# Second attention of a two-layer transformer kernel: row sums by the exponentials' accumulator, later projections, masked queries on GpSimd

## The chip, the cores and the metric

The kernel runs on one core of a Trainium2 chip. The metric is the device time of one execution in microseconds (us). The kernel before takes 2906.33 us (median of three, 2905.99 to 2908.69).

## What is computed

Two layers on x of 32 x 256 tokens x 128. Each layer adds attention and a feed-forward part (mixture of experts) of the normalised input to the residual. The change touches only the second layer's attention: 16 heads of 8 channels, causal, with a bias that falls with distance.

```python
q, k, v = (proj(q_w), proj(k_w), proj(v_w))
scores = jnp.einsum('bhid,bhjd->bhij', q, k) / scale
scores = scores - distance[None] * _slopes(N_HEADS)[:, None, None]
scores = jnp.where(causal[None, None], scores, -jnp.inf)
attn = jax.nn.softmax(scores, axis=-1)
out = jnp.einsum('bhij,bhjd->bhid', attn, v)
out = out.transpose(0, 2, 1, 3).reshape(b, l, D_MODEL)
return out @ o_w
```

## The kernel before

The program has four stages, one after the other: the first feed-forward part, the first attention, the second layer's experts, and the second attention, in which the experts' rows are also gathered and added. Everything is 32-bit floating point.

The second attention goes over 32 batches (sequences). A batch is eight units: two halves of 128 queries times four sets of four heads. Units 0 to 3 are narrow (the first 128 queries see 128 keys), units 4 to 7 wide (256 keys). Four units of one half make a group, whose context is gathered in one bank, O_ps. Five queues run beside one another, and each walks the same hand-written list of steps s (STEPS); in a step each does its part for a different unit, and semaphores hold them together:

- TensorE in step s: turn(s-1) transposes the exponentials (L1478, four transposes narrow, eight wide), value(s-2) multiplies them with v into columns 0 to 127 of O_ps (L1496) and with a table of ones into columns 128 to 255, which gives the row sums, turned and repeated over each head's channels (L1500), score(s+1) makes the scores (L1466), then comes a projection if the list has one.
- VectorE in step s: at s % 4 == 2 it divides a finished group: reciprocal of the sums (L1405), product (L1409). Then four minimum passes over the scores of unit s, which add the bias and give the negated scores and their minimum (L1419, each followed by a read of the accumulator), then the copy of the first half of the transposed unit s-1 (L1427). After an output projection it adds the total (L1434).
- ScalarE in step s: four exponentials of unit s (L1388), for wide units the copy of the second transposed half of s-1 (L1395), then it empties the projection bank: four masked copies of the queries, one per head position (L1367), kT (L1368), or v (L1377).
- GpSimd: indirect gathers of the experts' rows (L1335), the weighting and two sums (L1348, L1352, L1357). The last of them waits until the output projection two batches back was added.
- SyncE: loads of the transposed input (behind the v projection two batches back), stores of the output.

All projections share one bank, M_ps, in the order of job_list: q and k of the next batch at step 8b+1, v at 8b+2, the output projection of the batch before at 8b+3. Each waits until the bank was emptied of the one before (spare_free).

The lines of the list and of the division:

```python
job_list += [(UB * b + 1, "qk", b + 1), (UB * b + 2, "v", b + 1)]
job_list += [(UB * b + 3, "out", b - 1)]
dve.reciprocal(rinv[g % 2][:, :], O_ps[:, P:2 * P]).then_inc(inverted, 1)
```

Of the kernel before, what the change touches and what calls it, by code (L numbers as in the profile page):

```python
# [31 lines left out]
P = 128  # L32
S = 256
D = 128
H = 16
C = 8
# [25 lines left out]
def program(nc, io, nb, cap):  # L62
# [5 lines left out]
    with ctx:  # L68
# [434 lines left out]
        with ExitStack() as pm:  # L503
# [10 lines left out]
            UB = 8  # L514
# [575 lines left out]
        v_of = [sb(f"v1_heads{i}", [P, KT, 4, D]) for i in range(2)]  # L1090
        one_of = sb("ones_heads", [P, 4, 32])
        zeros_set = sem("zeros_set")
        ones_set = sem("ones_set")
        alibi_built = sem("alibi_built")

        with ExitStack() as pc:
# [27 lines left out]
            with nc.Block() as block:  # L1124
# [93 lines left out]
                def _(pool):  # L1218
# [3 lines left out]
                    for i in range(2):  # L1222
                        pool.memset(v_of[i][:, :, :, :], 0.0).then_inc(zeros_set, 1)
                    pool.memset(one_of[:, :, :], 0.0).then_inc(zeros_set, 1)
                    pool.wait_ge(zeros_set, 3)
                    for i in range(4):
                        pool.memset(one_of[:, i, C * i:C * i + C], 1.0).then_inc(ones_set, 1)
                    for h in range(H):
# [9 lines left out]
        with ExitStack() as pb:  # L1238
# [14 lines left out]
            xt = [sbb(f"xt1_{i}", [P, S]) for i in range(2)]  # L1253
            q_of = [sbb(f"q1_heads{i}", [P, 4, S]) for i in range(2)]
            kT = [sbb(f"kT1_{i}", [P, S]) for i in range(2)]
# [4 lines left out]
            rinv = [sbb(f"rinv1_{i}", [P, P]) for i in range(2)]  # L1260
            ctxT = [sbb(f"ctxT1_{i}", [P, S]) for i in range(2)]
# [14 lines left out]
            moved1 = semb("probsT_second_half_moved")  # L1276
            valued = semb("values_ready")
            inverted = semb("inverse_sums_ready")
            normed = semb("context_ready")
            spare_full = semb("spare_full")  # L1280
            spare_free = semb("spare_free")
            rows_weighted = semb("expert_rows_weighted")
            one_added = semb("first_expert_added")
# [15 lines left out]
            for b in range(nb + 1):  # L1299
                if b + 1 < nb:  # L1300
                    job_list += [(UB * b + 1, "qk", b + 1), (UB * b + 2, "v", b + 1)]
                if b >= 1:
                    job_list += [(UB * b + 3, "out", b - 1)]
            job_no = {(name, b): n + 1 for n, (_, name, b) in enumerate(job_list)}
            jobs_at = {}
            for s, name, b in job_list:
                jobs_at.setdefault(s, []).append((name, b))
            STEPS = range(-2, UB * nb + 7)

# [21 lines left out]
            def _(pool):  # L1331
                def gather(b):
                    for i in range(2):
                        for k in range(2):
                            pool.indirect_dma_start(out=expert_rows[b % 2][:, i, k, :], out_offset=None, in_=expert_out,  # L1335
                                                    in_offset=bass.IndirectOffsetOnAxis(ap=slot_ids[:, 2 * b + i, k:k + 1], axis=0)
                                                    ).then_inc(gathered[b % 2], 16)

                gather(0)
                for b in range(nb):  # L1340
# [5 lines left out]
                    if b >= 1:  # L1346
# [5 lines left out]
                    pool.tensor_tensor(with_one[:, :, :], weighted[:, :, 0, :], residual[:, 2 * b:2 * b + 2, :],  # L1352
                                       ALU.add).then_inc(one_added, 1)
                    pool.wait_ge(one_added, b + 1)
                    if b >= 2:
# [5 lines left out]
            def _(act):  # L1361
                def move(name, b):
                    n = job_no[name, b]
                    if name == "qk":
                        act.wait_ge(spare_full, n)
                        for i in range(4):
                            act.mul(q_of[b % 2][:, i, :], M_ps[:, 0:S], cview["head_scale"][:, i:i + 1])  # L1367
                        act.copy(kT[b % 2][:, :], M_ps[:, S:2 * S]).then_inc(spare_free, 1)  # L1368
                    elif name == "v":
                        act.wait_ge(spare_full, n)  # L1370
                        if b < 2:
                            act.wait_ge(zeros_set, 3)
                        else:
                            act.wait_ge(valued, UB * (b - 1))
# [25 lines left out]
            def _(dve):  # L1400
                for s in STEPS:
                    if s >= 6 and s % 4 == 2 and s // 4 - 1 < 2 * nb:
                        g = s // 4 - 1
                        dve.wait_ge(valued, 4 * (g + 1))
                        dve.reciprocal(rinv[g % 2][:, :], O_ps[:, P:2 * P]).then_inc(inverted, 1)  # L1405
                        dve.wait_ge(inverted, g + 1)
                        if g >= 4:
                            dve.wait_ge(spare_full, job_no["out", g // 2 - 2])
                        dve.tensor_tensor(ctxT[g // 2 % 2][:, g % 2 * P:(g % 2 + 1) * P], O_ps[:, 0:P], rinv[g % 2][:, :],  # L1409
                                          ALU.mult).then_inc(normed, 1)  # L1410
# [27 lines left out]
            def _(pe):  # L1438
# [42 lines left out]
                def value(u):  # L1481
# [4 lines left out]
                    if i == 0 and g >= 1:  # L1486
                        pe.wait_ge(normed, g)
                    if u == 0:
                        pe.wait_ge(ones_set, 4)
                    if u % UB == 0:  # L1490
                        pe.wait_ge(spare_free, job_no["v", b])
                    n = half_of(u) + 1
                    for kt in range(n):
                        for j in range(4):
                            rows = slice(32 * j, 32 * j + 32)
                            pe.matmul(O_ps[rows, 0:P], v_of[b % 2][:, kt, i, rows], probsT[u % 3][:, kt, j, :],  # L1496
                                      start=(i == 0 and kt == 0), stop=(i == 3 and kt == n - 1), skip_group_check=True)
# [89 lines left out]
```

## Time and profile before

| | |
|---|---|
| median of three | 2906.33 us |
| profiled execution by itself | 2909.2 us |
| its span | 2907.5 us |
| mean granted clock of TensorE | 0.969 |
| busy: TensorE, VectorE, ScalarE, GpSimd | 90%, 66%, 55%, 21% |
| second attention | 2180 us to the end |

The page gives busy time and instructions by engine, the span in 40 slices with the granted clock of TensorE in tenths of full speed, and the chain of work that ended last. The chain can be read in order of time: each piece is what the end waited for at that time. The timeline shows every engine, with the idle time before an instruction and what ended it in brackets. A matmul in 32-bit is recorded as two instructions, a transpose as one.

### The profile page before, as it was taken

The numbers are of one execution on the slowest core, as the hardware profiler recorded it, in microseconds if no ns is written. First come the engines' busy times: TensorE is split into PE (matmuls) and PEld (weight loads), VectorE is DVE, ScalarE is ACT, GpSimd is POOL, SyncE is SP. The second block draws the span as 40 slices with busy tenths as digits, with TensorE's granted clock in tenths as the row PEclk, the third lists the DMA queues.
The fourth block names the chain that finished last, engine by engine and source line by source line (L and its number), as shares of the span: only waits on it lengthen the run. The fifth ranks groups of instructions, "written<-read, shape, count | busy, mean of one in ns | idle before, by whom it ended". The sixth has DMA issues, their size and how long they took to land. (4 is left out here: it accounts for less than half of the span.)

```text
span 2907.5 us, 102728 instructions
## 1 busy us (share of the span) xinstructions
PE 2604.1 (90%) x42000; PEld 1971.0 (68%) x42000; DVE 1924.4 (66%) x7310; ACT 1611.4 (55%) x3731; POOL 613.6 (21%) x632
## 2 busy tenths in 40 slices
PE   4999999799988999999999999499989999998998
PEld 3777777567767777777777777377766666666666
DVE  4887788467777777777777777211117777777777
ACT  1444444366666666666666665133327666767776
POOL 2445444300110000001111111400004223322230
PEclk9999999899999999999999999699999999999999
DMA  3212100166666666666666665222321001111110
GB/s 131 103 51 73 37 15 12 36 152 148 154 151 149 152 153 148 152 155 149 152 150 153 150 149 123 86 84 98 101 72 35 24 24 29 26 24 24 28 27 9
DMA packets 341502, 268.43 MB, mean 92 GB/s; under 512 B 24602, under 2 KB 328090, under 8 KB 339516
## 3 DMA queue, kind: packets, MB, share of 16 engines
q1 hardware_dynamic: 330556, 234.82, 31.4%
q0 software_dynamic: 10496, 27.28, 3.2%
q8 instruction: 323, 5.29, 0.8%
q14 instruction: 127, 1.04, 0.1%
HBM read 129.88 MB, written 132.14 MB: 90 GB/s over the span
## 5 line engine op out<-in xcount | busy, mean ns | idle before, releaser
L869 DVE CUSTOM_DVE_ANT_0 neg_scores<-scores,rel_bias 128x256 f32<-128x256 f32 x1024 | 373.4, 421 | 271.7 <-PE scores L1013 226.4
L1388 ACT ACTIVATE probs<-neg_scores,low 128x256 f32<-128x256 f32 (+1 forms) x1024 | 382.5, 446 | 211.6 <-DVE low L1419 187.4
L757 ACT ACTIVATE probs<-neg_scores,low 128x256 f32<-128x256 f32 x1024 | 436.8, 500 | 42.9 <-DVE low L869 41.8
L751 ACT COPY probsT_s<-probsT 128x512 f32<-128x512 f32 x256 | 150.3, 587 | 427.6 <-PE probsT L1025 427.6
L1419 DVE CUSTOM_DVE_ANT_0 neg_scores<-scores,alibi 128x256 f32<-128x256 f32 (+1 forms) x1024 | 304.8, 354 | 109.5 <-PE scores L1466 109.2
L1025 PE MATMUL probsT<-consts,probs 128*128 128x128 f32 x2048 | 332.7, 286 | 1.3 <-ACT probsT_s L751 0.7
L1025 PEld LDWEIGHTS probsT<-consts,probs 128*128 128x128 f32 x2048 | 229.1, 143 | 72.9 <-issue 59.4
L252 POOL TENSOR_TENSOR hid<-hid,gate_bc 128x512 f32<-128x512 f32 x160 | 205.4, 1284 | 275.8 <-DVE hid L407 257.3
L876 DVE COPY rel_s<-scores 128x768 f32<-128x768 f32 x256 | 244.0, 953 | 3.0 <-PE scores L1013 1.6
L1003 PE MATMUL scores<-k_sides,q_heads 32*128 32x256 f32 x2048 | 184.3, 429 | 55.6 <-DVE rel_s L876 54.1
L1478 PE MATMUL probsT<-consts,probs 128*128 128x128 f32 x1536 | 226.8, 285 | 3.7 <-ACT probs L1388 0.4
L1427 DVE COPY probsT_s<-probsT 128x512 f32<-128x512 f32 x256 | 175.9, 687 | 68.6 <-PE probsT L1478 68.4
L1041 PE MATMUL values<-probsT_s,v_heads 128*32 128x128 f32 x4096 | 216.1, 283 | 0.8 <-issue 0.8
L1188 ACT ACTIVATE he<-up,b1e 128x512 f32<-128x512 f32 (+1 forms) x192 | 112.0, 616 | 183.4 <-PE up L1166 183.2
L1478 PEld LDWEIGHTS probsT<-consts,probs 128*128 128x128 f32 x1536 | 172.7, 144 | 56.3 <-ACT probs L1388 39.0
L1045 PE MATMUL values<-probsT_s,ones_heads 128*32 128x128 f32 x4096 | 209.6, 276 | 0.0
L1213 DVE TENSOR_TENSOR ye<-down,b 128x512 f32<-128x512 f32 (+1 forms) x48 | 28.9, 603 | 253.0 <-PE down L1174 253.0
L712 POOL TENSOR_TENSOR scat_f<-dumpk,sk 128x8 f32<-128x8 f32 x16 | 3.1, 195 | 888.4 <-DVE dump_at L849 888.4
L275 ACT ACTIVATE th<-gate_up 128x512 f32<-128x512 f32 x160 | 95.8, 599 | 168.5 <-PE gate_up L464 166.7
L484 PE MATMUL ffn_down<-weights,hid 128*128 128x128 f32 x1280 | 184.0, 287 | 0.1
L484 PEld LDWEIGHTS ffn_down<-weights,hid 128*128 128x128 f32 x1280 | 156.8, 192 | 36.3 <-issue 27.7
L719 POOL DMA_INDIRECT packed<-xn,scat x128 | 124.2, 970 | 268.1 <-DVE low L869 243.8
(187 smaller groups left out, 5158.9 us busy)
## 6 DMA issues: line engine op xcount, KB each, us to landing
rel_rows<-rel_s SPq DMA_DIRECT2D x256, 192.0 KB
rel_bias<-rel_rows SPq DMA_DIRECT2D x256, 192.0 KB, 4.0
rel_rows<-rel_s SPq DMA_DIRECT2D x256, 128.0 KB
rel_bias<-rel_rows SPq DMA_DIRECT2D x256, 128.0 KB, 3.4
packed<-ffn_in SPq DMA_DIRECT2D x8, 1280.0 KB, 5.5
xe<-packed SPq DMA_DIRECT2D x16, 640.0 KB, 4.3
expert_out<-ye POOLq DMA_DIRECT2D x16, 640.0 KB, 6.9
xt<-xnT SPq DMA_DIRECT2D x64, 128.0 KB, 3.1
```

Of the source, the lines that this page charges most:

```text
L252: pool.tensor_tensor(hid[p % 2][:, k, :], hid[p % 2][:, k, :], gate_bc[m % 3][:, :], ALU.mult).then_inc(hid_done, 1)
L484: ins = pe.matmul(D_ps[p % 2][:, i * D:(i + 1) * D], hid[p % 2][:, k, i * P:(i + 1) * P], wview["wdown"][:, k * D:(k + 1) * D], start=(k = ...
L757: act.activation(probs[s % 2][:, j, :], neg[s % 2][:, j, :], ACT.Exp, bias=low[s % 3][:, j:j + 1], scale=-1.0).then_inc(exped, 1)
L869: dve.tensor_tensor_reduce(neg[s % 2][:, j, :], S_ps[:, 512 * j:512 * j + S], bias_of(s)[:, j, :], 1.0, 3e38, ALU.add, ALU.min, low[s % 3] ...
L876: dve.tensor_copy(rel_s[u % 2][:, :, :], S_ps[:, :].rearrange("p (j w) -> p j w", j=4)[:, :, S:S + 3 * R]).then_inc(rel_moved, 1)
L1003: ins = pe.matmul(S_ps[:, 512 * j:512 * j + S], q_of[b % 2][rows, i, qt * P:(qt + 1) * P], k_of[b % 2][rows, qt, :], start=True, stop=True)
L1025: ins = pe.transpose(PT_ps[:, j * P:(j + 1) * P], probs[u % 2][:, j, kt * P:(kt + 1) * P], ident)
L1041: pe.matmul(O_ps[rows, qt * P:(qt + 1) * P], v_of[b % 2][:, kt, i, rows], pt[:, j, :], start=(u % UB == 0 and kt == 0), stop=(i == 3 and k ...
L1045: ins = pe.matmul(O_ps[rows, S + qt * P:S + (qt + 1) * P], one_of[:, i, :], pt[:, j, :], start=False, stop=(i == 3 and kt == KT - 1), skip ...
L1388: act.activation(probs[s % 3][:, j, 0:w], neg[s % 3][:, j, 0:w], ACT.Exp, bias=low[s % 3][:, j:j + 1], scale=-1.0).then_inc(exped, 1)
L1419: dve.tensor_tensor_reduce(neg[s % 3][:, j, 0:w], S_ps[j][:, 0:w], alibi[:, 4 * j + i, S - w:S], 1.0, 3e38, ALU.add, ALU.min, low[s % 3][: ...
L1478: ins = pe.transpose(PT_ps[kt][:, j * P:(j + 1) * P], probs[u % 3][:, j, kt * P:(kt + 1) * P], ident)
```

## The change

1. The ones table, its memsets and the ones matmuls go. Each exponential gets accum_out, which leaves its row sum in a 128 x 4 x 4 tile of the group. Behind the copy of a group's last unit VectorE takes the reciprocal of 128x16 sums and widens them to 128x128 (each head's value repeated over its eight channels). TensorE turns this with one matmul against the identity into columns 128 to 255 of O_ps, behind the last values of the group. At the old place of the reciprocal stands a copy of these columns to SBUF; the product follows as before.
2. The v projection moves from step 8b+2 to 8b+3, the output projection from 8b+3 to 8b+5.
3. ScalarE copies the queries once (q_raw); GpSimd makes the four masked copies (query_heads), for batch 0 ahead of its first gather, for later ones behind with_one. The scores of a batch's first unit wait for q_ready.

```diff
-                job_list += [(UB * b + 1, "qk", b + 1), (UB * b + 2, "v", b + 1)]
+                job_list += [(UB * b + 1, "qk", b + 1), (UB * b + 3, "v", b + 1)]
-                job_list += [(UB * b + 3, "out", b - 1)]
+                job_list += [(UB * b + 5, "out", b - 1)]
...
+                def query_heads(b):
+                    pool.wait_ge(spare_free, job_no["qk", b])
+                    for i in range(4):
+                        ins = pool.tensor_scalar(q_of[b % 2][:, i, :], q_raw[:, :], cview["head_scale"][:, i:i + 1], None, ALU.mult)
+                    ins.then_inc(q_ready, 1)
+
+                query_heads(0)
                 gather(0)
...
+                    if b >= 1:
+                        query_heads(b)
                     pool.wait_ge(one_added, b + 1)
...
-                        for i in range(4):
-                            act.mul(q_of[b % 2][:, i, :], M_ps[:, 0:S], cview["head_scale"][:, i:i + 1])
+                        if b >= 1:
+                            act.wait_ge(q_ready, b)
+                        act.copy(q_raw[:, :], M_ps[:, 0:S])
...
+                        g, i = s // 4, s % 4
+                        if i == 0 and g >= 2:
+                            act.wait_ge(inverted, g - 1)
...
                             act.activation(probs[s % 3][:, j, 0:w], neg[s % 3][:, j, 0:w], ACT.Exp,
-                                           bias=low[s % 3][:, j:j + 1], scale=-1.0).then_inc(exped, 1)
+                                           bias=low[s % 3][:, j:j + 1], scale=-1.0,
+                                           accum_out=sums[g % 2][:, j, i:i + 1]).then_inc(exped, 1)
...
-                        dve.reciprocal(rinv[g % 2][:, :], O_ps[:, P:2 * P]).then_inc(inverted, 1)
-                        dve.wait_ge(inverted, g + 1)
+                        dve.tensor_copy(rinvT[:, :], O_ps[:, P:2 * P]).then_inc(inverse_moved, 1)
+                        dve.wait_ge(inverse_moved, g + 1)
...
+                        if u % 4 == 3:
+                            g = u // 4
+                            dve.wait_ge(exped, 16 * (g + 1))
+                            dve.reciprocal(rinv[:, :], sums[g % 2][:, :, :].rearrange("p j i -> p (j i)")).then_inc(one_inverse, 1)
+                            dve.wait_ge(one_inverse, g + 1)
+                            if g >= 1:
+                                dve.wait_ge(valued, 4 * g)
+                            dve.tensor_copy(rinv_c[:, :, :], rinv[:, :].unsqueeze(2).to_broadcast((P, H, C))).then_inc(inverted, 1)
...
                     if u % UB == 0:
                         pe.wait_ge(spare_free, job_no["qk", b])
+                        pe.wait_ge(q_ready, b + 1)
...
-                        for j in range(4):
-                            rows = slice(32 * j, 32 * j + 32)
-                            ins = pe.matmul(O_ps[rows, P:2 * P], one_of[:, i, :], probsT[u % 3][:, kt, j, :],
-                                            start=False, stop=(i == 3 and kt == n - 1), skip_group_check=True)
+                    if i == 3:
+                        pe.wait_ge(inverted, g + 1)
+                        ins = pe.matmul(O_ps[:, P:2 * P], rinv_c[:, :, :].rearrange("p h c -> p (h c)"), ident, start=True, stop=True)
                     ins.then_inc(valued, 1)
```

## Rows read from the trace of the kernel before

**Rows 1.** The page, part 2: TensorE's granted clock in 40 slices.
```profile
PEclk9999999899999999999999999699999999999999
```
**Rows 2.** Chain in order of time, longest pieces: start us, us, what.
```profile
2285.22 1.15 PE projected L1454 x4
...
2868.85 1.15 PE projected L1454 x4
```
**Rows 3.** The same chain from 2485 to 2545 us, all pieces.
```profile
2495.75 1.13 PE probsT L1478 x8
2496.88 0.36 PE values L1496 x8
2497.24 0.22 PE values L1500 x8
...
2497.89 0.43 PE scores L1466 x8
2498.32 1.02 PE probsT L1478 x8
...
2500.79 0.59 PE probsT L1478 x4
...
2502.82 0.63 PE projected L1445 x2
...
2507.79 0.44 PE probsT L1478 x4
...
2508.80 0.69 PE scores L1466 x8
...
2517.27 1.13 PE probsT L1478 x8
...
2530.93 1.17 PE scores L1466 x8
...
2540.30 1.13 PE probsT L1478 x8
```
**Rows 4.** Timeline, one batch: start us, us, engine, line, out<-in, [idle before <-releaser].
```profile
2504.04 1.28 ACT L1388 ACTIVATE probs<-neg_scores,low 128x128 f32<-128x128 f32 x4 [1.50 <-DVE low L1419]
...
2505.23 1.54 ACT L1367 ACTIVATE q_heads<-projected,consts 128x256 f32<-128x256 f32 x4
...
2507.08 0.71 PE L1449 MATMUL projected<-weights,xt 128*128 128x128 f32 x4 [1.75 <-ACT kT L1368]
...
2513.81 0.95 DVE L1405 RECIPROCAL rinv<-values 128x128 f32<-128x128 f32 x1
...
2514.11 1.12 PE L1478 MATMUL probsT<-consts,probs 128*128 128x128 f32 x8
...
2514.79 0.29 DVE L1409 TENSOR_TENSOR ctxT<-values,rinv 128x128 f32<-128x128 f32 x1
...
2515.00 0.41 DVE L1419 CUSTOM_DVE_ANT_0 neg_scores<-scores,alibi 128x256 f32<-128x256 f32 x1
...
2515.34 0.08 DVE L1419 DVE_READ_ACCUMULATOR2_ANT low<- 128x1 f32 x1
2515.34 0.42 DVE L1419 CUSTOM_DVE_ANT_0 neg_scores<-scores,alibi 128x256 f32<-128x256 f32 x1
...
2515.52 1.71 ACT L1388 ACTIVATE probs<-neg_scores,low 128x256 f32<-128x256 f32 x4 [0.99 <-DVE low L1419]
```
**Rows 5.** Groups by line and shape: count, busy us, mean ns, idle before.
```profile
L1395 ACT COPY probsT_s<-probsT 128x512 f32<-128x512 f32 x128 | 72.1, 563 | 0.7 <-PE probsT L1478 0.7
...
L829 DVE RECIPROCAL gk<-den 128x4 f32<-128x4 f32 x16 | 2.9, 179 | 0.5
```
**Rows 6.** Timeline of ScalarE in the first stage, two small instructions.
```profile
328.32 0.21 ACT L297 ACTIVATE ex<-gap 128x4 f32<-128x4 f32 x1
328.42 0.20 ACT L298 ACTIVATE sg<-logit 128x4 f32<-128x4 f32 x1
```
**Rows 7.** Timeline of GpSimd in the experts' stage, sixteen tensor_scalar.
```profile
1856.09 14.65 POOL L1229 TENSOR_SCALAR alibi<-consts 128x256 f32<-128x256 f32 x16
```

More of the change, by code:

```diff
@@ L1090, in program @@
         v_of = [sb(f"v1_heads{i}", [P, KT, 4, D]) for i in range(2)]
-        one_of = sb("ones_heads", [P, 4, 32])
         zeros_set = sem("zeros_set")
-        ones_set = sem("ones_set")
         alibi_built = sem("alibi_built")
@@ L1223, in _ @@
                         pool.memset(v_of[i][:, :, :, :], 0.0).then_inc(zeros_set, 1)
-                    pool.memset(one_of[:, :, :], 0.0).then_inc(zeros_set, 1)
-                    pool.wait_ge(zeros_set, 3)
-                    for i in range(4):
-                        pool.memset(one_of[:, i, C * i:C * i + C], 1.0).then_inc(ones_set, 1)
                     for h in range(H):
@@ L1254, in program @@
             q_of = [sbb(f"q1_heads{i}", [P, 4, S]) for i in range(2)]
+            q_raw = sbb("q1_raw", [P, S])
             kT = [sbb(f"kT1_{i}", [P, S]) for i in range(2)]
@@ L1259, in program @@
             probsT = [sbb(f"probsT1_s{i}", [P, KT, 4, P]) for i in range(3)]
-            rinv = [sbb(f"rinv1_{i}", [P, P]) for i in range(2)]
+            sums = [sbb(f"sums1_{i}", [P, 4, 4]) for i in range(2)]
+            rinv = sbb("rinv1", [P, H])
+            rinv_c = sbb("rinv1_c", [P, H, C])
+            rinvT = sbb("rinv1_T", [P, P])
             ctxT = [sbb(f"ctxT1_{i}", [P, S]) for i in range(2)]
@@ L1277, in program @@
             valued = semb("values_ready")
+            one_inverse = semb("inverse_sums_of_heads")
             inverted = semb("inverse_sums_ready")
+            inverse_moved = semb("turned_inverse_moved")
             normed = semb("context_ready")
@@ L1281, in program @@
             spare_free = semb("spare_free")
+            q_ready = semb("query_heads_ready")
             rows_weighted = semb("expert_rows_weighted")
@@ L1307, in program @@
                 jobs_at.setdefault(s, []).append((name, b))
-            STEPS = range(-2, UB * nb + 7)
+            STEPS = range(-2, UB * nb + 8)
             block = pb.enter_context(nc.Block())
@@ L1365, in move @@
                         act.wait_ge(spare_full, n)
-                        for i in range(4):
-                            act.mul(q_of[b % 2][:, i, :], M_ps[:, 0:S], cview["head_scale"][:, i:i + 1])
+                        if b >= 1:
+                            act.wait_ge(q_ready, b)
+                        act.copy(q_raw[:, :], M_ps[:, 0:S])
                         act.copy(kT[b % 2][:, :], M_ps[:, S:2 * S]).then_inc(spare_free, 1)
@@ L1371, in move @@
                         if b < 2:
-                            act.wait_ge(zeros_set, 3)
+                            act.wait_ge(zeros_set, 2)
                         else:
@@ L1404, in _ @@
                         dve.wait_ge(valued, 4 * (g + 1))
-                        dve.reciprocal(rinv[g % 2][:, :], O_ps[:, P:2 * P]).then_inc(inverted, 1)
-                        dve.wait_ge(inverted, g + 1)
+                        dve.tensor_copy(rinvT[:, :], O_ps[:, P:2 * P]).then_inc(inverse_moved, 1)
+                        dve.wait_ge(inverse_moved, g + 1)
                         if g >= 4:
                             dve.wait_ge(spare_full, job_no["out", g // 2 - 2])
-                        dve.tensor_tensor(ctxT[g // 2 % 2][:, g % 2 * P:(g % 2 + 1) * P], O_ps[:, 0:P], rinv[g % 2][:, :],
+                        dve.tensor_tensor(ctxT[g // 2 % 2][:, g % 2 * P:(g % 2 + 1) * P], O_ps[:, 0:P], rinvT[:, :],
                                           ALU.mult).then_inc(normed, 1)
@@ L1487, in value @@
                         pe.wait_ge(normed, g)
-                    if u == 0:
-                        pe.wait_ge(ones_set, 4)
                     if u % UB == 0:
@@ L1495, in value @@
                             rows = slice(32 * j, 32 * j + 32)
-                            pe.matmul(O_ps[rows, 0:P], v_of[b % 2][:, kt, i, rows], probsT[u % 3][:, kt, j, :],
-                                      start=(i == 0 and kt == 0), stop=(i == 3 and kt == n - 1), skip_group_check=True)
-                        for j in range(4):
-                            rows = slice(32 * j, 32 * j + 32)
-                            ins = pe.matmul(O_ps[rows, P:2 * P], one_of[:, i, :], probsT[u % 3][:, kt, j, :],
-                                            start=False, stop=(i == 3 and kt == n - 1), skip_group_check=True)
+                            ins = pe.matmul(O_ps[rows, 0:P], v_of[b % 2][:, kt, i, rows], probsT[u % 3][:, kt, j, :],
+                                            start=(i == 0 and kt == 0), stop=(i == 3 and kt == n - 1), skip_group_check=True)
+                    if i == 3:
+                        pe.wait_ge(inverted, g + 1)
+                        ins = pe.matmul(O_ps[:, P:2 * P], rinv_c[:, :, :].rearrange("p h c -> p (h c)"), ident, start=True, stop=True)
                     ins.then_inc(valued, 1)
```

## The prediction

> **What bounds the kernel now.** I read the page first: the clock line, which stays at nine tenths and over in the last quarter [rows 1]. The second attention, which alone is changed, fills the last quarter: from the first projection at 2180 us to the end. Then the chain of the whole span: the same output projection stands in it at 2285.22 and, 26 batches later, at 2868.85 [rows 2], so a batch of eight units takes (2868.85 - 2285.22) / 26 = 22.45 us. Then one batch of the chain in order of time [rows 3]; the time from the start of one transposition of a unit to the next is a step. From unit 6 of a batch at 2495.75 to unit 6 of the next at 2517.27 it is 21.52 us. With units counted 0 to 7 and steps named by the unit that is transposed, step 6 takes 2.57 (to 2498.32), step 7 2.47 (to 2500.79), steps 0 and 1 7.0 (to 2507.79), steps 2 to 4 6.3 (to 2514.11) and step 5 3.2 [rows 3, 4].
>
> TensorE sets steps 6, 7, 0 and 2 to 4 nearly alone: its pieces follow one another in the chain. Step 7, for instance, is 1.02 (eight transposes) + 0.36 + 0.22 + 0.22 + 0.22 (values and ones, two key halves) + 0.43 (scores) = 2.47 [rows 3]. Step 1 is long because the v projection waits 1.75 us for the copies of ScalarE (four masked queries, 1.54 us, then kT) [rows 4]. Step 5 is set by VectorE: the reciprocal starts at 2513.81 and the next unit's minimum pass only at 2515.00, 1.19 us later [rows 4]. After each such row I ask what would be late next, for the gain ends there.
>
> The difference between 21.52 and 22.45 is the clock: in every second batch TensorE shows a stretch at its lower level (1.2 GHz), right behind the idle 1.75 us before the v projection. The scores of one unit then take 1.17 instead of 0.69 [rows 3]. The batch after the one above takes 23.03 (2517.27 to 2540.30), so some 1.5 us per pair, 0.75 per batch.
>
> **Part 1, the ones matmuls.** They go, 0.22 us of TensorE for each key half in the chain [rows 3]. Four narrow units have one half, four wide ones two: 12 x 0.22 = 2.6 us per batch. In their place comes one full matmul per group of four units; the two of the v projection with their issue take 0.71 [rows 4], so about 0.3 each, 0.6 per batch. Net -2.0 us of TensorE.
>
> **Part 2, the row sums.** Each of the 32 exponentials of a batch gets an accumulator read on ScalarE. The trace has none there, and this is the price on which everything hangs. Call it a, per exponential, on ScalarE's throughput. Bounds: on VectorE each minimum pass is followed by such a read of 0.08, and the next pass starts at the same instant, 2515.34 [rows 4]: a = 0 from below. From above, the dearest small ScalarE instruction (128x4) takes 0.21 by itself: a = 0.21 [rows 6]. In between, two such small instructions back to back start 0.10 apart [rows 6]. I take 0.10, since the read is to be expected as an instruction of its own of that size in the same queue. A gain below nothing is excluded: no work of ScalarE's exponential goes away.
>
> **Part 3, the division.** VectorE loses two reciprocals of 128x128 per batch (0.95 each) and gets, per group, a reciprocal of 128x16 (128x4 takes 0.18, 128x128 takes 0.95 [rows 4, 5]; with some 6.2 ns per element 0.25), a widening copy and a copy of the turned sums, each 128x128; their bounds are 0.18, the tiny instruction, and 0.95, the reciprocal, and I take the 0.29 of the product, which is nearest in shape and work [rows 4]. At the critical place, ahead of unit 6's and unit 2's minimum pass, 1.19 becomes 0.5 (a copy, and a product whose end overlaps the next pass). The other 0.5 stands behind the copy of unit 3's and 7's transpositions. The added matmul waits for it. Behind that wait on TensorE stand the scores of the unit two steps later and, through them, VectorE and ScalarE; but the sums are ready 1.2 us after the last minimum pass of that step, while the transposes (0.5 to 1.1, begun 0.6 behind that pass) and the values end later, so the wait costs nothing. If that cover were gone it would cost up to 0.5 twice a batch, 32 us in all.
>
> **Part 4, the queries.** ScalarE's four products (1.54 [rows 4]) become one copy, a quarter of that (0.38): -1.15 us per batch. GpSimd gets four tensor_scalar of 128x256. Sixteen of them took 14.65 us [rows 7], so 3.7 us per batch. They stand in its queue behind the gathers and the first two sums (some 7 us), so they are done about four steps after the queries' copy; scores need them six steps after, with some 5 us left over. What queues behind them (the second sum of the experts' rows) is needed 13 steps later. If the cover were gone, each us of lateness costs one per batch. Only at the start is it bare: the first scores wait for 0.38 + 3.7 instead of 1.54, so +2.3 us once; the first gathers move behind it and have time.
>
> **Part 5, the projections' places.** With v at step 3 of a batch, its wait for ScalarE (copy and kT, two copies of that size, 0.75 behind the exponentials of unit 2) lies beside transposes, values and scores (1.55). The 1.75 us go. The output projection moves with it and stands in step 4; the loads on SyncE's queue wait for v and out and are issued ten units ahead, two more matter not.
>
> **The sum.** For each step I take the largest of what TensorE, ScalarE and VectorE have to do and of the latency from scores to the transposition. That latency is, wide: 0.05 + 0.52 (first minimum to first exponential) + 1.71 + 0.05 = 2.33 and four reads; narrow 1.76 and four reads [rows 4]. The same method on the kernel before gives back the steps above within 0.1. After:
> - step 6: TensorE 1.13 + 0.58 (values of two key halves, 0.36 + 0.22) + 0.43 = 2.1, latency 2.4 + 4a: **2.8**
> - step 7: TensorE 2.0, ScalarE (copy 0.56 [rows 5], four narrow exponentials) 1.95 + 4a: **2.35**
> - steps 0 and 1: TensorE 2.85 (with the q and k projection) + 1.3: **4.2**; ScalarE 3.75 + 8a hides
> - step 2: TensorE 2.1, ScalarE (0.75 + 1.28 + gaps) + 4a: **2.5**
> - step 3: TensorE 1.55, ScalarE and latency 1.8 + 4a: **2.2**
> - steps 4 and 5: TensorE 3.1 (with the added matmul and the output projection) + 2.4: **5.5**; VectorE 2.0 + 2.9 and ScalarE 5.0 + 4a hide
>
> Together 19.55 us per batch against 22.45, and the clock's 0.75 is in this difference: I count it as gained, because the idle piece ahead of the lower clock goes and no idle piece in my table is over 0.7. So 2.9 x 31.5 batches = -91, +2.3 at the start, -1 at the end (shorter division), -89.5. The profiled execution took 2909.2 by itself (its span 2907.5), 2.9 more than the median of 2906.33; 2909.2 - 89.5 - 2.9 gives **2817**. By the ends of a: at 0 the steps are 2.4, 2.05, 4.15, 2.2, 1.7, 5.5 = 18.0, so 2768; at 0.21 ScalarE has 15.4 us of its own work and 32 x 0.21 = 6.7, 22.1, so 2897.
>
> **A rule that speaks against it.** The widening copy on VectorE goes from SBUF to SBUF while GpSimd makes queries; the trace of before has no such pair in this stage, VectorE's copies here come from PSUM. Were the copy held for a whole GpSimd instruction (0.85 to 0.92 [rows 7]) once a batch, it would fall in step 3, where 0.5 of it is hidden: up to 0.4 x 32 = 13 us. The Trainium skill (SBUF — State Buffer, "Who interferes with whom") says that a VectorE copy in a two-port mode and GpSimd lock each other out of a shared port pair for a whole instruction. No row here shows it; by it the sum would be at most 2830, inside the range.
>
> **The rivals.**
> - *The read is hidden* (a under 0.05), as on VectorE: 2768 to 2792. For it the row of VectorE's reads; against it that small ScalarE instructions do take their 0.10.
> - *ScalarE becomes the bound* (a from 0.14 to 0.21): 2845 to 2897. TensorE then waits for exponentials in nearly every step. For it: ScalarE's own work is 15.4 us per batch already (four wide exponentials at 1.71, four narrow at 1.28 less the overlaps, four copies at 0.6, queries, kT and v 1.2).
> - *Slower than before*: the read overlaps neither the exponential before it (0.10 lost) nor the one behind (0.21 [rows 6]): a = 0.31, 15.4 + 9.9 = 25.3 us per batch, 2.9 x 31.5 = +91, 2997. It decides from a = 0.22 on, where ScalarE's 15.4 + 32a passes 22.45. Against it: neighbouring instructions on ScalarE overlap [rows 6].
> - *It doesn't do what it says*: the queries come late, or the lower clock stays. TensorE has 17.4 us of work in 19.6, 89%, where it has 19.4 in 22.45 now, 86%; so I doubt it, but falls of the clock may go on at 0.75 per batch: +24, 2841. Late queries by over 5 us would give back 1 us of each batch per us.
>
> **How the numbers follow.** Chances: my case (a from 0.05 to 0.14, 2792 to 2845) 0.45; hidden read 0.24; ScalarE bound 0.17; slower 0.07; queries late or clock low for long stretches, 2870 to 2910, 0.07. The range runs from 2768 to 2880: it leaves out the slower case, half of the last one and the dear end of ScalarE's. A measurement of this kernel tells 0.2%, 6 us, from no change. Faster: 0.45 + 0.24 + 0.17 + 0.04 = 0.90, same 0.03, slower 0.07.
>
> **What would show it.** Right: reads on ScalarE, with exponentials of a wide unit standing 0.50 apart instead of 0.40; no idle time of TensorE before the v projection; 1.2 us less between VectorE's copies around unit 6, no reciprocal of 0.95; a batch of 19 to 20 us; the wait for the turned sums absent from the list of waits. Wrong: exponentials 0.6 apart; TensorE waiting for GpSimd's queries; VectorE's small copy far over 0.3; a clock line in the last quarter lower than before.

## The result

The changed kernel takes 2797.7 us (median of four, 2797.55 to 2800.91) against 2906.16 (four, 2905.67 to 2908.69): a ratio of 0.9628, 95% interval 0.9611 to 0.9644, 108 us or 3.7% faster. The prediction was 2817 us with a range from 2768 to 2880. The profiled execution has a span of 2799.2.

The page of the changed kernel: span, busy times, TensorE's clock in 40 slices.

```profile
span 2799.2 us, 98114 instructions
...
PE 2515.8 (90%) x39056; PEld 1887.1 (67%) x39056; DVE 1912.2 (68%) x7438; ACT 1668.0 (60%) x4659; POOL 730.2 (26%) x755
...
PEclk9999999989999999999999999979999899999999
```

Against [rows 1] the clock line looks alike, since a slice of it rounds. The table by stretches of the second attention shows the difference (us from the start, length, busy times of TensorE, weight loads, VectorE, ScalarE and GpSimd, granted clock, DMA share, GB/s), first the kernel before, then the changed one:

```profile
2400.00:2500.00 100.00, 91.14 (x1424) 65.50 (x1425) 76.34 (x344) 70.60 (x192) 31.20 (x35) 0.95 0.11 29
```

```profile
2400.00:2500.00 100.00, 93.18 (x1179) 63.33 (x1177) 88.54 (x431) 92.61 (x383) 53.62 (x59) 1.00 0.11 28
```

The clock is 1.00 where the kernel before has 0.95 in the same stretch, and three engines are now about equally busy. One batch of the chain in order of time answers to [rows 3]:

```profile
2488.59 1.13 PE probsT L1502 x8
2489.72 0.57 PE values L1518 x16
2490.30 0.43 PE scores L1490 x8
2490.73 0.59 PE probsT L1502 x4
2491.32 0.57 PE values L1518 x16
2491.89 0.42 PE values L1522 x2
...
2493.80 0.44 PE probsT L1502 x4
...
2495.11 0.63 PE probsT L1502 x4
...
2498.41 1.08 ACT probs L1402 x4
2499.50 0.04 issue
2499.54 1.10 PE probsT L1502 x8
...
2502.70 0.87 PE probsT L1502 x8
...
2506.38 1.09 ACT probs L1402 x4
2507.47 0.04 issue
2507.51 1.13 PE probsT L1502 x8
```

From the transposition of unit 7 at 2488.59 to the next at 2507.51 it is 18.92 us. The values of unit 7 take 0.57 without ones (L1518), then stands the one added matmul (L1522, 0.42). No piece of VectorE's division is left in the chain; before, the reciprocal stood in it ahead of unit 6. The chain now leaves TensorE ahead of the transpositions of units 4 and 7 (2499.54 and 2507.51), where it goes through ScalarE's exponentials. 22.45 - 18.92 = 3.53 us per batch, by 31.5 batches 111, less 2.6 lost at the start: that is the 108.

How the comparisons below are made. The experiments were measured in four series, each beside the kernel before: e1 to e4; e5, e6, e7 and e9; e10, e11 and e8; e12. In three of these, with nine of the twelve runs, some steps of each batch are longer for every kernel whose trace was kept, and the kernel before takes 2992 to 2999 us instead of 2902 to 2906. I call this the long step. It lies where GpSimd issues its four gathers or just behind: steps 5 and 6 with the projections at their old places, steps 7 and 0 at the new ones (in e7 nearly all of it in step 7). With the lower clock around it a batch is 2 to 5 us longer in the mean. So the totals of these runs can't be set against the 2797.7. The last batch that is followed by another (from the transposition of unit 0 to the next unit 0) has no gathers in it and no long step, and in the series without long steps it is as long as the others (18.92 in the changed kernel, in e10 and in e11). Its length, read from TensorE's timeline, is what I compare. It is one batch of one execution per kernel; where the same kernel was profiled again it came out the same within 0.01 us (18.92 three times, 18.17 in e4 and e12). The columns are the units' steps, from the start of one transposition to the next, and the batch, in us; the last column is TensorE's granted clock in that batch:

| kernel | 0 | 1 | 2 | 3 | 4 | 5 | 6 | 7 | batch | clock |
|---|---|---|---|---|---|---|---|---|---|---|
| before | 3.00 | 3.91 | 3.38 | 2.21 | 2.43 | 3.16 | 2.50 | 2.47 | 23.06 | 0.93 |
| before, batch at full clock | 3.00 | 3.91 | 2.30 | 1.88 | 2.31 | 3.16 | 2.50 | 2.47 | 21.52 | 1.00 |
| changed | 2.98 | 1.48 | 2.16 | 2.27 | 2.99 | 2.24 | 2.74 | 2.06 | 18.92 | 1.00 |
| e1, before with reads | 3.00 | 4.74 | 3.38 | 2.25 | 2.31 | 3.27 | 2.51 | 2.47 | 23.93 | 0.93 |
| e2, before, positions | 3.00 | 1.66 | 2.88 | 1.80 | 2.85 | 2.74 | 2.50 | 2.46 | 19.89 | 1.00 |
| e3, before, queries | 3.00 | 2.72 | 2.29 | 1.88 | 2.31 | 3.16 | 2.50 | 2.47 | 20.33 | 1.00 |
| e12, changed without reads | 2.98 | 1.47 | 2.16 | 1.90 | 2.99 | 2.18 | 2.43 | 2.06 | 18.17 | 1.00 |
| e5, changed, old positions | 2.98 | 2.40 | 2.08 | 2.26 | 2.71 | 2.53 | 2.55 | 2.05 | 19.56 | 1.00 |
| e6, changed, ScalarE's queries | 2.98 | 1.47 | 3.10 | 1.97 | 2.99 | 2.25 | 2.73 | 2.06 | 19.55 | 1.00 |
| e7, changed with ones too | 3.42 | 1.53 | 2.36 | 2.26 | 3.21 | 2.62 | 2.79 | 2.50 | 20.69 | 1.00 |
| e9, changed, more ScalarE | 3.05 | 1.61 | 2.46 | 2.35 | 2.99 | 2.54 | 2.82 | 2.41 | 20.22 | 1.00 |
| e8, output at step 7 | 2.98 | 1.48 | 2.16 | 2.27 | 2.44 | 2.79 | 2.61 | 1.98 | 18.71 | 1.00 |

### The profile page after: what moved, and what is told of

Read it like the earlier page. It is cut to its first block and busy times, and to the rows that moved or that the text cites. A ratio compares the mean times of both kernels' runs of the same rounds, so it can differ in the third digit from the quotient of the medians.

```text
span 2799.2 us, 98114 instructions
## 1 busy us (share of the span) xinstructions
PE 2515.8 (90%) x39056; PEld 1887.1 (67%) x39056; DVE 1912.2 (68%) x7438; ACT 1668.0 (60%) x4659; POOL 730.2 (26%) x755
## 3 DMA queue, kind: packets, MB, share of 16 engines
q14 instruction: 138, 1.13, 0.1%
## 5 line engine op out<-in xcount | busy, mean ns | idle before, releaser
L1402 ACT ACTIVATE probs<-neg_scores,low 128x256 f32<-128x256 f32 (+1 forms) x1024 | 453.1, 443 | 54.6 <-DVE low L1434 52.0
L1402 ACT ACTIVATION_READ_ACCUMULATOR probs<-neg_scores,low 128x1 f32 x1024 | 191.2, 187 | 0.0
```

## The experiments

In the cuts of the edits below, allocations and the length of the list of steps are left out. Theory: the gain is the wait before the v projection with the lower clock behind it, the ones matmuls, and the reciprocal ahead of units 2 and 6, less a small price of the accumulator reads, which counts only where ScalarE ends the chain. Rivals: the reads are free or dear; the ones matmuls were hidden; the clock does not hang on the wait.

### e1: the reads alone

```diff
-  bias=low[s % 3][:, j:j + 1], scale=-1.0).then_inc(exped, 1)
+  bias=low[s % 3][:, j:j + 1], scale=-1.0,
+  accum_out=sums[s // 4 % 2][:, j, s % 4:s % 4 + 1]).then_inc(exped, 1)
```

> The kernel before, with the row sums also written by the exponentials' accumulator, and not used. Theory: a read adds 0.09 us to each exponential and TensorE's chain already ends on exponentials in the steps of units 6, 4, 5 and 1, so some 4 x 0.37 us per batch come on top: 2906 + 45, 2935 to 2965. Rival: ScalarE is busy only 70% of this stage, so 32 x 0.09 = 3 us per batch disappear in its idle time: under 2916.

Measured: 3016.47 us against 2998.8 beside it, ratio 1.006 (1.0031 to 1.009), and 23.93 - 23.06 = +0.87 per batch. Both batches hold a stretch at the lower clock. Neither expectation is met: the price is there, at somewhat over half the 1.5 per batch of the theory. Nearly all of it (0.83) is in step 1, behind which ScalarE still has the four query products; in the steps of units 4 and 6, where I had put a third of it each, TensorE and VectorE hide it.

### e2: the positions alone

```diff
-  job_list += [(UB * b + 1, "qk", b + 1), (UB * b + 2, "v", b + 1)]
+  job_list += [(UB * b + 1, "qk", b + 1), (UB * b + 3, "v", b + 1)]
-  job_list += [(UB * b + 3, "out", b - 1)]
+  job_list += [(UB * b + 5, "out", b - 1)]
```

> The kernel before with only the projections moved (v three units and the output five units into a batch). Theory: TensorE's wait of 1.75 us before the v projection goes, but the four products of ScalarE (1.54 us) then delay the next exponentials, which gives some of it back; with the idle piece the stretch at the lower clock goes too (0.75 per batch): -1.9 us per batch, 2845 (2830 to 2865), the granted clock of the stage 1.00. Rival, the clock does not depend on that wait: clock as before at 0.95 to 0.97 and 2870 or more. Rival, the products bound the step as much as the wait did: 2890 or more.

Measured: 2961.55 us, ratio 0.9877 (0.9825 to 0.9929), a batch of 19.89 at a clock of 1.00: -1.63 against a batch at full clock, -2.56 against the mean of 22.45. The theory had -1.9 with the clock's part, so by this one batch it holds and is too small. Step 1 falls from 3.91 to 1.66, step 2 grows by 0.58 (the query products now delay unit 3's exponentials), and step 5 falls too, from 3.16 to 2.74, which I had not foreseen; that more of VectorE's division then lies beside TensorE's work is likely, but not shown. The total does not confirm it: ratio and clock are those of the rival (0.9877 of 2906 is 2870, and its 30 batches have 18 falls of the clock). TensorE's granted clock, read batch by batch, tells more than the mean: in the kernel before all 18 falls of the clock in its batches 1 to 30 (counted from 0) come in steps 1 and 2, right behind the wait before the v projection; in e2 all 18 come in steps 7 and 0, at the long step, and none behind the v projection. So moving the projections took the falls away from that place, and the long step, which the kernel of the result did not have, made others.

### e3: the queries alone

```diff
-  for i in range(4):
-      act.mul(q_of[b % 2][:, i, :], M_ps[:, 0:S], cview["head_scale"][:, i:i + 1])
+  if b >= 1:
+      act.wait_ge(q_ready, b)
+  act.copy(q_raw[:, :], M_ps[:, 0:S])
```

with query_heads on GpSimd as in the change.

> The kernel before with only the masked queries moved to GpSimd. Theory: the wait before the v projection becomes 1.15 us shorter, 0.6 instead of 1.75, and the lower clock goes with it; +2.3 us at the start: 2906 - 37 - 24 + 2 = 2847. Without the clock's part 2871. Rival: GpSimd is late, or its work slows VectorE: 2895 or more, with TensorE or VectorE idle until GpSimd.

Measured: 2951.29 us, ratio 0.9842 (0.9791 to 0.9893), a batch of 20.33 at a clock of 1.00: -1.19, all in step 1 (3.91 to 2.72), and -2.12 with the clock. Without the clock the theory holds to 0.04 in this batch. The total is 47.5 us shorter, not the 59 expected: here too the 30 batches have 18 falls of the clock, all of them in steps 5 to 7, at the long step, and none behind the wait of 0.6 us that is left before the v projection. In this stage no engine waits for GpSimd's queries but once, at the start.

### e4 and e12: the changed kernel without the reads

```diff
-  bias=low[s % 3][:, j:j + 1], scale=-1.0,
-  accum_out=sums[g % 2][:, j, i:i + 1]).then_inc(exped, 1)
+  bias=low[s % 3][:, j:j + 1], scale=-1.0).then_inc(exped, 1)
```

The sums are set to one on GpSimd once, so the division does nothing and the output is not the reference's.

> The changed kernel without the accumulator reads: the sums are constants set once, so the division is by ones and the output is not the reference's; all else stays. Theory: the read costs only where the latency from scores to transposes or ScalarE's queue ends last (the steps of units 6, 7, 2 and 3), about 1.0 us of 18.9 per batch: 2766 (2755 to 2775). Rival: TensorE bounds it all the same, over 2790. Rival: ScalarE bounds every step, then all 32 x 0.09 = 3.0 us per batch come back: 2702.

> The changed kernel without the accumulator reads once more (the sums are constants, the output is not the reference's), for a chip without the long step. Theory, by the undisturbed steps of the run e4_after_no_reads: 2.98 + 1.47 + 2.16 + 1.90 + 2.99 + 2.18 + 2.42 + 2.06 = 18.16 us per batch against 18.92, so 2797.7 - 0.76 x 31.5 = 2774. Rival: the disturbed steps hid a gain of ScalarE's, then all 3.0 us per batch come back, 2703.

Both series had the long step: 2926.27 us (ratio 0.9756, 0.9676 to 0.9837) and 2927.92 (0.9775, 0.9745 to 0.9804), so the totals decide nothing, and 2774 was not seen. The undisturbed batch is 18.17 in both: the reads cost 0.75 us of 18.92. TensorE's timeline of e12, its steps of units 5, 6 and 7:

```profile
2892.30 1.09 PE L1506 MATMUL probsT<-consts,probs 128*128 128x128 f32 x8
2894.73 1.12 PE L1506 MATMUL probsT<-consts,probs 128*128 128x128 f32 x8 [0.17 <-ACT probs L1405]
2896.79 0.65 PE L1506 MATMUL probsT<-consts,probs 128*128 128x128 f32 x4
```

Unit 6's step is 2.43 instead of 2.74, and TensorE's wait in it is 0.17 instead of 0.54; unit 3's is 1.90 instead of 2.27. Step 7, where I had put 0.3, does not move. By 31.5 batches that is 24 us. The rival with all 3 us is out, and so is the one of over 2790: 2797.7 less 24 is 2774, by this estimate.

### e5, e6, e7: one part taken back from the changed kernel

e5 is the diff of e2 the other way round, e6 that of e3. e7 puts the ones matmuls back ahead of the added one (with their table, not shown):

```diff
+  for j in range(4):
+      rows = slice(32 * j, 32 * j + 32)
+      ins = pe.matmul(O_ps[rows, P:2 * P], one_of[:, i, :], probsT[u % 3][:, kt, j, :],
+                      start=False, stop=(i == 3 and kt == n - 1), skip_group_check=True)
```

> The changed kernel with the projections back at their old places (v two units into a batch, the output three). Theory: TensorE waits for the copies of queries and kT again, 0.7 us instead of 1.9 since the masked queries are gone, some 0.5 us per batch: 2815 (2805 to 2825), the clock still 1.00 as the idle piece is short. Rival: the lower clock comes back with the wait and it costs 0.5 + 0.75 per batch, 2838 or more. Rival: the places are worth nothing once the queries are on GpSimd, under 2802.

> The changed kernel with the four masked query products back on ScalarE. Theory: ScalarE gets 1.15 us per batch behind the exponentials of unit 2, and unit 3's exponentials end last there: +1.0 to 1.15 per batch, -2.3 at the start: 2829 (2820 to 2835). Rival: with the v projection a unit later there is room, under 2810.

> The changed kernel with the ones matmuls put back beside the new sums (their result is overwritten). Theory: 2.6 us more of TensorE per batch, of which the waits for exponentials in the steps of units 6 and 3 hide some 0.6: +2.0 per batch, 2861 (2850 to 2872). Rival: ScalarE bounds the stage now and TensorE's work is hidden: under 2820.

Measured: e5 2904.36 (ratio 0.972, 0.9658 to 0.9782), e6 2963.62 (0.9907, 0.9878 to 0.9935), e7 2963.79 (0.9899, 0.9855 to 0.9943). By the batch: old positions +0.64, with the clock still at 1.00, as expected (0.5); ScalarE's queries +0.63, between the 1.0 of the theory and the rival's 0.4, since 0.94 more in step 2 comes back as 0.30 less in step 3; ones matmuls +1.77 against 2.0. In e7 the chain shows them at their full price beside the values (L1527, 0.22 for each key half):

```profile
2940.24 0.36 PE values L1523 x8
2940.59 0.22 PE values L1527 x8
2940.81 0.22 PE values L1523 x8
2941.03 0.22 PE values L1527 x8
2941.25 0.43 PE scores L1493 x8
```

So of the 2.6 us of these matmuls 0.8 are hidden now, most of it in steps 3 and 6, where TensorE waits for exponentials.

Two of these totals say more than their batches. e5 and e6 were measured side by side and have the same undisturbed batch (19.56 and 19.55), but e5 takes 2904 us and e6 2964. They differ in the projections' places and in which engine masks the queries. e2 and e3, measured side by side, show the same: e2 has the shorter undisturbed batch (19.89 against 20.33) and takes 10 us more. Where the long step occurs, kernels with the new places lost more to it (3.2 to 5.2 us per batch in the mean) than those with the old ones (1.9 to 3.6). So the gain of 3.7% is one for executions without the long step; with it the changed kernel's gain is probably smaller, since e4 and e12 had only 2.4 and 2.2% even without the reads.

Taken back one by one the parts are worth 0.64 (places), 0.63 (queries) and 1.77 (ones) less 0.75 for the reads, 2.29 us per batch, and the clock's part is some 0.9. Of the 3.53 this leaves some 0.3 for the new division and for what the parts give only together. No run takes the division back alone, so its own share is not shown.

### e9: more of ScalarE's time

```diff
   accum_out=sums[g % 2][:, j, i:i + 1]).then_inc(exped, 1)
+  act.copy(small[:, s, j, :], cview["head_scale"][:, :])
```

> The changed kernel with one more small ScalarE instruction (a copy of 128x4) behind each exponential, 0.10 us each, as if the read cost 0.19. Theory: ScalarE's queue becomes the bound in nearly every step, 15.4 + 32 x 0.19 = 21.5 plus some waits, 22.0 us per batch against 18.9: 2896 (2880 to 2906). Rival: the slope stays that of the other direction, about 1 us per batch per 0.09: 2835.

Measured: 3012.32 us, ratio 1.0054 (1.0024 to 1.0084), with the long step; a batch of 20.22, +1.30. The theory's 22.0 is refuted. ScalarE's timeline of e9 (start us, length):

```profile
2980.03 0.51 ACT L1403 ACTIVATE probs<-neg_scores,low 128x256 f32<-128x256 f32 x1
2980.44 0.19 ACT L1403 ACTIVATION_READ_ACCUMULATOR probs<-neg_scores,low 128x1 f32 x1
2980.53 0.18 ACT L1406 COPY small<-consts 128x4 f32<-128x4 f32 x1
2980.61 0.51 ACT L1403 ACTIVATE probs<-neg_scores,low 128x256 f32<-128x256 f32 x1
```

The added copy moves the next exponential by 0.09 (0.58 apart, and 0.49 in the changed kernel below), 2.9 us per batch, of which 1.3 arrive. The rival is met: it had 1.2 per batch. The reason is the term for ScalarE's own work, next section.

### e10, e11, e8: the changed kernel again, without gathers, and with a later output projection

e11 leaves the gathers out from the third batch on. e8:

```diff
-  job_list += [(UB * b + 5, "out", b - 1)]
+  job_list += [(UB * b + 7, "out", b - 1)]
```

> The changed kernel once more, on the chip of the next two. In the runs so far one step of each batch, the one in which GpSimd issues its four gathers, is 2 to 4 us longer than on the first chip, whatever the kernel. Theory, that this belongs to the chip: on such a chip the step of unit 7 takes 4 to 5 us instead of 2.06, the other steps are as on the first chip, 2797.7 + 32 x 2.7 = 2884 (2870 to 2900); on a chip like the first 2798. Rival, that the edited kernels made it: 2798 on any chip.

> The changed kernel without the gathers of experts' rows from the third batch on (the rows of the first two are used again, so the output is not the reference's). Theory, that the gathers hold VectorE and TensorE: the long step goes, unit 7 back at 2.1 us, 2797 on any chip. Rival, the loads and stores that SyncE issues at the same time do it: as the run before, 2884 on such a chip. On a chip like the first both give 2797.

> The changed kernel with the output projection two units later still, at step 8b+7, where TensorE waits 0.55 us for the exponentials of unit 7. Theory: steps 4 and 5 lose its 0.64 us on TensorE, but ScalarE is busy there and ends the chain 0.2 us later: -0.2 to -0.4 per batch, 6 to 13 us faster than the run of the changed kernel beside it. Rival, TensorE alone sets steps 4 and 5: -0.64, 20 us faster. Rival, the total's sum on VectorE now stands ahead of the group's inverse and costs what was won: same within 3 us.

This series had no long step: e10 2806.01 us (ratio 0.9672, 0.9654 to 0.969, to 2902.54 beside it), e11 2800.44 (0.9642, 0.9625 to 0.966), e8 2795.84 (0.9634, 0.9617 to 0.9651). The changed kernel's gain is 3.3% here against 3.7% in the result, with intervals that do not meet, though from the third batch on e10's trace has the same batches as the first one (18.92); what the slower executions (2803 to 2810) lost is in no trace. So a ratio from another series is good to some 0.5% only. e11 could not tell gathers from loads, and says only that gathers cost nothing per batch where there is no long step. e8 is 10 us faster than e10, with intervals that just part, and its batch is 0.21 shorter (18.71). That is 7 us by 31.5 batches, of the size that the theory gave. The place is another: steps 4 and 5 gain nothing together (5.23 both times), for TensorE, free of the projection, then waits 0.42 for unit 6's exponentials, and the gain comes in steps 6 and 7 (2.74 and 2.06 become 2.61 and 1.98), where the projection fills a wait. Of the kernels that compute the whole output e8 has the shortest batch.

## Why the prediction was right

**The bounds of the kernel before.** The reading that the v projection's wait and VectorE's reciprocal are on the path held for the wait: e2 and e3 shorten step 1 by 2.25 and 1.19. The reciprocal is gone from the chain in the changed kernel, but no run took it out alone.

**The clock** [rows 3]. The mechanism was right, the count was not. The fall does not come in every second batch: of batches 1 to 30 of the kernel before 18 have it (23.1 us), 12 have not (21.5 or 21.6), so it costs 0.9 us per batch and not 0.75. The sum goes from 22.45 and is not touched by this. In the changed kernel no fall comes in batches 1 to 30, nor in e8, e10 and e11 (all without the long step), and TensorE's idle pieces there are at most 0.6 us, but for two of 0.7 and 0.8. In e2, e3 and e5, which have one part each of what shortens the wait, none comes behind the v projection. Where the wait stays, in e1 (2.1 us and more), 16 of 23 falls come there. So the falls behind the v projection hang on that wait; why they come in some batches and not in others of the kernel before stays open.

**Part 1.** 2.0 us net; e7 measured 1.77 for the ones alone, which take 2.6 by duration. The added matmul takes 0.42 of the chain and not 0.3, so by duration TensorE's net is 1.8.

**Part 2, the read.** Taken at 0.10, measured at 0.09. ScalarE's timeline in the changed kernel:

```profile
2486.47 0.51 ACT L1402 ACTIVATE probs<-neg_scores,low 128x256 f32<-128x256 f32 x1 [0.19 <-DVE low L1434]
...
2486.97 0.49 ACT L1402 ACTIVATE probs<-neg_scores,low 128x256 f32<-128x256 f32 x1
2487.37 0.19 ACT L1402 ACTIVATION_READ_ACCUMULATOR probs<-neg_scores,low 128x1 f32 x1
2487.46 0.49 ACT L1402 ACTIVATE probs<-neg_scores,low 128x256 f32<-128x256 f32 x1
...
2488.45 0.56 ACT L1410 COPY probsT_s<-probsT 128x512 f32<-128x512 f32 x1
2488.91 0.40 ACT L1402 ACTIVATE probs<-neg_scores,low 128x128 f32<-128x128 f32 x1
```

Exponentials of a wide unit stand 0.49 apart; before it was (1.71 - 0.50) / 3 = 0.40 [rows 4]. The read itself is 0.19, half of it beside its neighbours. This is like the two small instructions of [rows 6] and not like VectorE's read [rows 4]. The nearest row was the right one.

**Part 3.** VectorE's small steps around unit 7, from its timeline:

```profile
2489.90 0.24 DVE L1446 RECIPROCAL rinv<-sums 128x16 f32<-128x16 f32 x1
...
2490.18 0.23 DVE L1450 COPY rinv_c<-rinv 128x128 f32<-128x128 f32 x1
...
2492.34 0.29 DVE L1420 COPY rinv_T<-values 128x128 f32<-128x128 f32 x1
...
2492.67 0.29 DVE L1424 TENSOR_TENSOR ctxT<-values,rinv_T 128x128 f32<-128x128 f32 x1
2492.88 0.28 DVE L1434 CUSTOM_DVE_ANT_0 neg_scores<-scores,alibi 128x128 f32<-128x128 f32 x1
```

The reciprocal takes 0.24 (0.25), the two copies 0.23 and 0.29 (0.29), and from the first copy to the minimum pass it is 0.54 where it was 1.19 [rows 4]. The sign that the prediction gave for this, 1.2 us less, does not follow from its own sum (1.19 to 0.5) and did not come. The wait of the added matmul is in no list of waits: the inverse is ready at 2490.41, the matmul starts at 2491.82.

**The port rule.** The 13 us did not come, but not because the rule fails. In the changed kernel the widening copy never meets GpSimd's queries by more than 0.03 us: in each batch one copy starts as the last product ends (at 2499.13, with the products done at 2499.15) and takes 0.23 like the others. Where other runs put the copy beside GpSimd, it was held. In all 39 cases, from five runs, in which GpSimd's weighting or a sum ran on for more than 0.15 us behind the copy's start, the copy took 0.27 to 0.80 us instead of 0.23 and ended 0.08 to 0.10 behind GpSimd's instruction. One of them, in e12:

```profile
2240.41 0.73 POOL L1363 TENSOR_TENSOR with_one<-weighted_rows,residual 128x256 f32<-128x256 f32 x1
2240.45 0.77 DVE L1454 COPY rinv_c<-rinv 128x128 f32<-128x128 f32 x1
```

Of 36 such meetings with a product, most of them in e8, the copy took 0.27 to 0.35 in 32 and ended 0.08 behind the product; in two it took 0.43 and 0.47 and ended in the middle of one, and in two it was not held. So the trace agrees with the rule of the Trainium skill (SBUF — State Buffer, "Who interferes with whom") that the two engines hold each other up, and for GpSimd's sums that it is to the end of the instruction. That the changed kernel's copy meets only the last 0.03 us is luck of its place. What a held copy costs per batch no run isolates.

**Part 4.** GpSimd's four products take 3.62 (3.7), at 2495.53 to 2499.15, and the scores that need them, unit 0's, come at 2506.47, so there were 7 us left, not 5. At the start the first scores come 6.6 us behind the first projection instead of 4.0, +2.6 (2.3):

```profile
2177.13 3.63 POOL L1343 TENSOR_SCALAR q_heads<-q_raw,consts 128x256 f32<-128x256 f32 x4 [9.40 <-ACT kT L1379]
...
2180.90 0.81 PE L1490 MATMUL scores<-kT,q_heads 32*128 32x128 f32 x8 [4.56 <-POOL q_heads L1343]
```

**Part 5.** No wait before the v projection is left in the list of waits. What stands there instead is what the sum named next, exponentials:

```profile
PEld probsT L1502 <- ACT probs L1402: 70.1, 126, 1.1
...
PE probsT L1502 <- ACT probs L1402: 31.3, 63, 0.8
```

**The sum** was 0.63 us per batch too long, 19.55 against 18.92, and so the gain 89.5 instead of 108. Step by step, predicted and measured: 6: 2.8 and 2.74; 7: 2.35 and 2.06; 0 and 1: 4.2 and 4.46; 2: 2.5 and 2.16; 3: 2.2 and 2.27; 4 and 5: 5.5 and 5.23. The mis-sized term is ScalarE's work in steps 7 and 2, which TensorE sets in truth. I took four exponentials at their joint duration (1.71 and 1.28, [rows 4]), which holds the tail of the last one, and the copies at theirs; but each next instruction starts before that tail is over. By starts, from the timeline above: a wide unit takes 2488.45 - 2486.47 = 1.98 with its reads, a narrow one 1.55, a copy 0.46, queries and kT 0.53, v 0.40. That is 4 x 1.98 + 4 x 1.55 + 4 x 0.46 + 0.93 = 16.9 with reads and 14.0 without, where I had 15.4. The same was done to TensorE: eight transposes take 1.03 and 0.97 by starts in steps 4 and 5, where I took 1.13 each. Steps 0 and 1 were too short by 0.26, of which the added matmul is 0.12 and step 1 (1.48 instead of 1.3) most of the rest. So in part the errors cancel.

With 14.0 + 32 x 0.18 = 19.8 the queue explains e9's 20.22, where my 15.4 gave 21.2 and with waits 22.0. So "ScalarE becomes the bound" was a cheaper rival than I made it.

At a = 0 the sum gave 18.0, and e12 measured 18.17. That is luck more than method: steps 0 and 1 are 0.3 longer and steps 4 and 5 0.3 shorter than it said. From a = 0 to 0.10 the sum grows by 1.55, in steps 6, 7, 2 and 3; the measured price of the reads is 0.75, in steps 6 (0.31) and 3 (0.37), and nothing in 7 and 2. The size of one read was right, the number of places where it counts was twice too large.

## What to carry to other kernels

Before adding an operation that the trace does not show, look for the row of the same engine that is nearest in size, and take the distance between starts, not the duration: for ScalarE's accumulator read the former is 0.09 us and the latter 0.19. For the same reason add up a queue's work by starts; four joined instructions carry one tail that the next one hides, and here these tails made 1.4 us of a 19 us batch. And where a wait on TensorE is followed by a stretch at its lower clock, count both: shortening the wait by 1.19 us gave 2.1 per batch, in a batch that nothing else disturbed. A small copy on VectorE beside GpSimd's work should be looked for in the trace by its length: here 0.23 us alone and up to 0.80 beside a sum of GpSimd.

## What had not been expected of the hardware

In the series with the long step engines pause while GpSimd issues its gathers. In e7 VectorE stands still before a minimum pass, and in 28 batches it goes on within 0.13 us of the end of GpSimd's next instruction, the weighting; the scores it would read are there. In e2 it is the same within 0.2 us. In e3 it is TensorE that pauses first, up to 1.1 us between the matmuls of one group, and VectorE waits for it; in e7 TensorE has such gaps too. VectorE's timeline in e7 (start us, us, engine, line, in brackets the idle time before it and what ended it):

```profile
2850.35 0.29 DVE L1437 CUSTOM_DVE_ANT_0 neg_scores<-scores,alibi 128x128 f32<-128x128 f32 x1 [4.12 <-remote]
```

And GpSimd's timeline in e7 around it:

```profile
2844.43 1.02 POOL L1339 DMA_INDIRECT expert_rows<-expert_out,slot_ids  x1 [0.15 <-issue]
...
2848.26 0.94 POOL L1339 DMA_INDIRECT expert_rows<-expert_out,slot_ids  x1 [0.30 <-issue]
2849.22 1.06 POOL L1359 TENSOR_TENSOR weighted_rows<-expert_rows,slot_w 128x512 f32<-128x512 f32 x1
```

The pass starts at 2850.35, when the weighting that began at 2849.22 is over. The pauses follow the gathers: with the projections at their old places they are in steps 5 and 6, with the new ones in steps 7 and 0. In the last batches, where GpSimd has no gathers left and SyncE only stores, the long step ends. It comes and goes on the same chip: e10, e11 and e8 ran without it, e12, on that chip later, with it. So my expectation that it belongs to a chip was wrong. The rival, that the edited kernels made it, is out too: the kernel before is some 90 us slower beside them, and e8 and e11 are edited and free of it. What makes it, and whether the gathers alone or the loads that SyncE issues beside them, stays open: the run without gathers fell into a series that had no long step. How fast the changed kernel itself is where the long step occurs was not measured.
